# The second layer's state space preparation moves into the first layer's attention

## The reference, cut to what matters

```python
def attention(h, wq, wk, wv, wo):            # layer 0, 32 heads of 64, 8 key heads; in _L0_ffn_ref
    ...
    scores = jnp.einsum('bhqd,bhkd->bhqk', q, k) / jnp.sqrt(jnp.float32(D))
    ...
    attn = jax.nn.softmax(scores, axis=-1)
    out = jnp.einsum('bhqk,bhkd->bhqd', attn, v)
    ...
    return out @ wo

def _ssm_forward(hidden_states, z, in_proj_w, conv_w, conv_b, x_proj_w, dt_proj_w, dt_proj_b, A_log, D):
    x = jnp.einsum('ed,bld->bel', in_proj_w, hidden_states)     # layer 1; hidden_states is the context
    ...                                                          # causal convolution over 4 places
    u = jax.nn.silu(xc + conv_b[None, :, None])
    x_dbl = jnp.einsum('ke,bel->bkl', x_proj_w, u)
    dt_lo = x_dbl[:, :DR]
    Bm = x_dbl[:, DR:DR + DS]
    Cm = x_dbl[:, DR + DS:]
    delta = jax.nn.softplus(jnp.einsum('er,brl->bel', dt_proj_w, dt_lo) + dt_proj_b[None, :, None])
    A = -jnp.exp(A_log)
    ...                                                          # the scan
```

## Time and profile before

| what | us |
|---|---|
| median of three runs (lowest, highest) | 2777.11 (2775.63, 2784.5) |
| profiled execution | 2792.75 |
| its span | 2791.5 |
| TensorE busy in the span | 2100.1 (75%) |
| VectorE busy | 1581.8 (57%) |
| ScalarE busy | 1107.5 (40%) |
| GpSimd busy | 1007.5 (36%) |

### The profile page before, as it was taken

One profiled execution on the slowest core, in us unless ns is written; L12 is line 12 of the kernel. 1 busy time (PEld: TensorE's weight loads), 2 busy tenths in 40 slices (PEclk: granted clock), 3 DMA queues, 4 the chain that ended last, 5 costly groups with the idle time before them and its releaser, 6 DMA issues. The chain is left out here.

```text
span 2791.5 us, 35700 instructions
## 1 busy us (share of the span) xinstructions
PE 2100.1 (75%) x12825; PEld 1478.7 (53%) x12872; DVE 1581.8 (57%) x3073; ACT 1107.5 (40%) x2234; POOL 1007.5 (36%) x1048
## 2 busy tenths in 40 slices
PE   6676735999974888856525688878999968797755
PEld 2333313776754777743303344546888845554444
DVE  6877674444444555545687655544546555455466
ACT  3255415555432444422264144542444434312534
POOL 2766501666536656651152033321233212100012
PEclk8756767999987999988757878978999989799787
DMA  3222100000004444420100000011000000010000
GB/s 134 72 57 56 39 21 28 18 12 22 9 1 155 159 159 155 155 71 15 45 0 37 2 3 3 3 54 46 1 1 1 1 1 2 2 39 7 2 37 15
DMA packets 48431, 114.59 MB, mean 41 GB/s; under 512 B 5472, under 2 KB 18144, under 8 KB 46976
## 3 DMA queue, kind: packets, MB, share of 16 engines
q1 hardware_dynamic: 46720, 108.10, 12.0%
q0 software_dynamic: 1536, 4.20, 0.5%
HBM read 100.09 MB, written 11.14 MB: 40 GB/s over the span
## 5 line engine op out<-in xcount | busy, mean ns | idle before, releaser
L1717 POOL TENSOR_SCALAR l0f_probs<-l0f_probs,l0f_tot 128x128 f32<-128x128 f32 (+1 forms) x256 | 190.8, 766 | 134.1 <-DVE l0f_tot L1671 133.9
L1939 PE MATMUL ps<-l0f_xh,l0f_wh 128*128 128x256 f32 x480 | 147.9, 308 | 49.6 <-DVE l1x_dBu L594 28.3
L1200 DVE TENSOR_REDUCE l2a_a_max<-ps 128x6 f32<-128x768 f32 x128 | 119.4, 954 | 87.6 <-PE ps L1052 87.0
L2889 POOL TENSOR_TENSOR l2x_probs<-l2x_probs,l2x_rc 128x512 f32<-128x512 f32 x64 | 66.6, 1041 | 265.1 <-DVE l2x_rc L2804 265.1
L1256 POOL TENSOR_SCALAR_AFFINE_SELECT l2a_a_probs<-l2a_a_probs 128x256 f32<-128x256 f32 (+1 forms) x192 | 88.5, 485 | 172.8 <-ACT l2a_a_probs L1162 150.9
L2054 POOL TENSOR_TENSOR l0f_wl<-l0f_raw,l0f_wh 128x1024 fp32r<-128x1024 f32 x60 | 141.8, 2376 | 17.3 <-ACT l0f_wh L1979 17.2
L1941 PE MATMUL ps<-l0f_xh,l0f_wl 128*128 128x256 f32 x480 | 139.8, 291 | 0.0
L1601 ACT ACTIVATE l0f_probs<-ps,l0f_neg 128x128 f32<-128x128 f32 (+1 forms) x256 | 104.6, 426 | 88.3 <-DVE l0f_neg L1661 88.3
L1940 PE MATMUL ps<-l0f_xl,l0f_wh 128*128 128x256 f32 x480 | 139.5, 291 | 0.0
L619 POOL TENSOR_TENSOR l1x_y<-l1x_y,l1x_hc 128x512 f32<-128x512 f32 x64 | 80.8, 1284 | 126.4 <-DVE l1x_hc L610 126.4
L1939 PEld LDWEIGHTS ps<-l0f_xh,l0f_wh 128*128 128x128 f32 x480 | 95.4, 199 | 57.4 <-issue 31.8
(11 more groups left out here) (758 smaller groups left out, 5919.6 us busy)
## 6 DMA issues: line engine op xcount, KB each, us to landing
l0f_raw<-in_e_l0f SPq DMA_DIRECT2D x60, 512.0 KB, 3.8
l0x_bc<-scratch_bc SPq DMA_DIRECT2D x32, 512.0 KB, 4.8
l0f_raw_d<-in_e_l0f SPq DMA_DIRECT2D x60, 256.0 KB, 3.7
scratch_rows<-zero SPq DMA_DIRECT2D x1, 3840.0 KB, 19.0
l0f_xb<-scratch_rows SPq DMA_DIRECT2D x15, 256.0 KB, 4.1
scratch_results<-l0f_yb SPq DMA_DIRECT2D x15, 256.0 KB, 4.4
l0f_slab<-in_g_l0f SPq DMA_DIRECT2D x8, 448.0 KB, 3.5
l1f_raw<-in_w_l1f SPq DMA_DIRECT2D x1, 3072.0 KB, 10.2
```

What stands on the lines that cost most here:

```text
L1200: dve.tensor_reduce(M[:, 2 * half:2 * half + 2, j, :], src.rearrange("p a (c n) -> p a c n", c=NB_), AX.X, ALU.max).then_inc(*unit_max.tick())
L1717: last = pool.tensor_scalar(pr[:, u % 3, a, r], pr[:, u % 3, a, r], tot[:, u % 3, qt, a:a + 1], None, ALU.mult)
L1939: pe.matmul(out, hi, xh[:, j % 2, c, :], start=c == 0, stop=False)
```

## The change

`prepare` no longer runs as a stage. It only makes the buffers and signals, and the work is cut into pieces that the loops of `l0f_attention` call in their steps. The pieces with a matmul also take a place in the ring, as a use "P" between A and V. The pieces by step:

| steps | TensorE | ScalarE | VectorE |
|---|---|---|---|
| before -8 | | Exp of A | negate A, halve the convolution's weights |
| 0 to 3 | context projection | copy | |
| 5 to 12 | | tanh in 10 | convolution, one instruction per step |
| 13, 16 | | tanh in 14 | (tanh + 1) times x/2 |
| 18, 19 | low rank rows | copy | |
| 20 to 23 | B and C rows | | split into three parts, seven instructions |
| 25 to 28 | time steps | | bias |
| 30 to 34 | | Abs 30, 31; Exp 32, 33; both Ln 34 | |
| 36 to 39 | | | skip term and sum 36, 38; product 37, 39 |

The silu is formed as x/2 (1 + tanh(x/2)) with the halved weights instead of x / (1 + exp(-x)): Exp, add, reciprocal and product become tanh and one instruction. Abs, Exp and Ln work on halves of 1024 columns instead of quarters of 512. The buffers of the sum, u and the low rank rows now lie in buffers that the scan has anyway. The memsets and copies of GpSimd run behind its first two weight splits. One barrier goes.

```diff
+    INNER, LOW, ROWS, DT = range(4), range(18, 20), range(20, 24), range(25, 29)
+    def emptied(self, n):
+        for at, done in ((self.INNER, self.in_sb), (self.LOW, self.low_sb), (self.ROWS, self.bc_sb), (self.DT, self.dt_in)):
+            if n in at:
+                return done(n - at[0] + 1)
...
+        if n in (10, 14):
+            d = (n - 10) // 4
+            act.wait_ge(*self.conv(d + 1))
+            act.activation(self.dt[:, d], self.du[:, d], ACT.Tanh).then_inc(*self.tanh.tick())
...
+        if n == 34:
+            for d in range(2):
+                act.wait_ge(*ac(d + 4))
+                act.activation(self.dt[:, d], self.dt[:, d], ACT.Ln, bias=1.0).then_inc(*self.dt_ln.tick())
...
+        if n in (13, 16):
+            d = (n - 13) // 3
+            dve.wait_ge(*self.tanh(d + 1))
+            dve.scalar_tensor_tensor(self.du[:, d], self.dt[:, d], 1.0, self.du[:, d], ALU.add, ALU.mult).then_inc(*self.u_ok.tick())
...
+        if n in self.ROWS:
...
+            dve.wait_ge(*self.bc_ps(i + 1))
+            dve.wait_ge(*self.cleared(9))
+            dve.tensor_copy(hb, bank[0:96, :]).then_inc(*v.tick())
+            dve.wait_ge(*v.now())
+            dve.tensor_tensor(rest, bank[0:96, :], hb, ALU.subtract).then_inc(*self.bc_sb.tick())
+            dve.tensor_copy(out[0:16], hb[0:16])
+            dve.wait_ge(*self.bc_sb(i + 1))
+            dve.tensor_copy(mb, rest).then_inc(*v.tick())
...
-        scan.prepare()
-        l0f_attention(k, h, xT)
+        l0f_attention(k, h, xT, scan)
...
-        uses += [("A", g, i) for g, i in a_of(n)] + ([("V", n - 3, 0)] if 0 <= n - 3 < N else []) + [("O", g, i) for g, i in o_of(n)]
+        uses += [("A", g, i) for g, i in a_of(n)] + scan.uses(n) + ([("V", n - 3, 0)] if 0 <= n - 3 < N else []) + [("O", g, i) for g, i in o_of(n)]
...
                 for g, i in a_of(n):
                     project(g, i)
+                for u in scan.uses(n):
+                    scan.pe_step(n, ring(*u), ring_free(*u))
                 if 0 <= n - 2 < N:
                     turn(n - 2)
...
             high(0)
+            scan.act_first()
...
+                if scan.uses(n):
+                    scan.act_step(n, ring("P", n, 0))
                 if 0 <= n < N:
                     exponent(n)
+                if not scan.uses(n):
+                    scan.act_step(n, None)
                 if 0 <= n - 2 < N:
                     take_turned(n - 2)
...
                 if 0 <= n - 2 < N:
                     take_turned(n - 2)
+                scan.dve_step(n, ring("P", n, 0) if scan.uses(n) else None)
                 for g, i in o_of(n):
                     add(g, i)
```

More of the change, by code:

```diff
@@ L412, in __init__ @@
         self.bs = [sb("bst", [P, NB, S], BF16), sb("cst", [P, NB, S], BF16)]
[L414 to L443, removed]
@@ L444, in at_pe, with pe_step @@
+    def pe_step(self, n, bank, free):
+        k, pe, w = self.k, self.k.pe, self.w
+        pe.wait_ge(*free)
+        if n in self.INNER:
+            d, hf = divmod(n - self.INNER[0], 2)
+            if n == self.INNER[0]:
                 pe.wait_ge(*k.loaded(self.wname))
                 pe.wait_ge(*k.loaded("ctx"))
[L446 to L459, removed]
@@ L543, in prepare @@
-            at_pool()
[L544 to L547, removed]
+            pe.matmul(bank, w["inp"][:, d * P:(d + 1) * P], k.ctxT[:, hf * HALF:(hf + 1) * HALF], start=True, stop=True).then_inc(*self.in_ps.tick())
+        elif n in self.LOW:
+            hf = n - self.LOW[0]
+            pe.wait_ge(*self.u_ok(2))
+            for c in range(2):
+                last = pe.matmul(bank[0:8, :], w["xw"][:, c, 0:8], self.flat(self.du, c)[:, hf * HALF:(hf + 1) * HALF], start=c == 0, stop=c == 1)
+            last.then_inc(*self.low_ps.tick())
+        elif n in self.ROWS:
+            hf, z = divmod(n - self.ROWS[0], 2)
+            pe.wait_ge(*self.cleared(9))
+            for c in range(2):
+                last = pe.matmul(bank[0:96, :], self.wr[:, c, z, :], self.flat(self.du, c)[:, hf * HALF:(hf + 1) * HALF], start=c == 0, stop=c == 1)
+            last.then_inc(*self.bc_ps.tick())
+        else:
+            d, hf = divmod(n - self.DT[0], 2)
+            pe.wait_ge(*self.low_sb(hf + 1))
+            pe.matmul(bank, w["dtw"][:, d * P:(d + 1) * P], self.low[:, hf * HALF:(hf + 1) * HALF], start=True, stop=True).then_inc(*self.dt_ps.tick())
@@ new lines, in act_first, with act_step @@
+    def act_first(self):
+        self.k.act.wait_ge(*self.k.loaded(self.wname))
+        self.k.act.activation(self.An[:, :, :], self.w["alog"], ACT.Exp).then_inc(*self.chain.tick())
+    def act_step(self, n, bank):
+        act, ac = self.k.act, self.chain
+        if n in self.INNER:
+            d, hf = divmod(n - self.INNER[0], 2)
+            act.wait_ge(*self.in_ps(n - self.INNER[0] + 1))
+            act.copy(self.xp[:, d, 2 * hf:2 * hf + 2, 3:3 + S], bank.rearrange("p (b s) -> p b s", s=S)).then_inc(*self.in_sb.tick())
+        if n in (10, 14):
+            d = (n - 10) // 4
+            act.wait_ge(*self.conv(d + 1))
+            act.activation(self.dt[:, d], self.du[:, d], ACT.Tanh).then_inc(*self.tanh.tick())
+        if n in self.LOW:
+            hf = n - self.LOW[0]
+            act.wait_ge(*self.low_ps(hf + 1))
+            act.copy(self.low[:, hf * HALF:(hf + 1) * HALF], bank[0:8, :]).then_inc(*self.low_sb.tick())
+        if n in (30, 31):
+            d = n - 30
+            act.wait_ge(*self.dt_in(2 * d + 2))
+            act.activation(self.dt[:, d], self.t(d), ACT.Abs).then_inc(*ac.tick())
+        if n in (32, 33):
+            d = n - 32
+            act.wait_ge(*ac(d + 2))
+            act.activation(self.dt[:, d], self.dt[:, d], ACT.Exp, scale=-1.0).then_inc(*ac.tick())
+        if n == 34:
+            for d in range(2):
+                act.wait_ge(*ac(d + 4))
+                act.activation(self.dt[:, d], self.dt[:, d], ACT.Ln, bias=1.0).then_inc(*self.dt_ln.tick())
```

159 lines of the change are left out of this document (77 added, 82 removed).

## The result

| what | us |
|---|---|
| before, median of 4 runs (lowest, highest) | 2778.66 (2775.63, 2784.5) |
| after, median of 4 runs (lowest, highest) | 2741.39 (2737.8, 2747.87) |
| ratio, 95% interval | 0.986 (0.9844 to 0.9876) |
| profiled execution after, its span | 2741.67, 2740.4 |

The changed kernel is 37 us faster. I had forecast 2731 us with a range of 2714 to 2750; the measured median lies 1.4 us above the narrower 2722 to 2740 that I had given to my own mechanism. Steps repeat from one execution to another to 0.05 us, except where TensorE's clock falls.

A forecast was written before the change was run, and what follows sets the result against it. Preparation was taken as a chain of engines waiting for each other, attention as bound by TensorE. 70.8 us go and 25.1 come back (17.8 - 4.1 + 5.2 + 2.3 + 3.9): -45.7 from 2777.1, so 2731 us, range 2714 to 2750.

The forecast's parts named there:

- old stage gone: Preparation ahead of the attention: nothing else runs there, so all of its 70.8 us lie on the path and go.
- context projection in 0 to 3, less the waits filled: Attention steps 0 to 3: four projections of 0.89 us each, with 2.0 us taken as filling TensorE's waits; +1.5 us.
- low rank pieces in 18, 19, less the wait filled: Attention steps 18 and 19: two pieces of 1.78 us each on TensorE, filling a wait of 0.96; +2.6 us.
- time step pieces in 25 to 28, less the waits of 24 and 27: Attention steps 25 to 28: pieces of 0.89 us each on TensorE, filling waits of 0.22 and 0.96; +2.4 us.
- waits for the bank: Back projection waits for the piece's bank: 1.35 us in steps 20, 21, 22 and 0.55 in 27, 28; +5.2 us.
- Ln ahead of the copy in 34: Step 34, ScalarE: table load and two Ln delay the copy of the turned probabilities, so TensorE waits; +2.3 us.
- lock between VectorE and GpSimd: Steps 8, 11, 40 and 17: VectorE instructions with two SBUF operands block GpSimd's multiplications through a shared port pair; +3.9 us.
- TensorE pays for each record: Attention, bound by TensorE: 20 inserted matmuls are 40 records of 0.444 us at full clock, all counted; +17.8 us.
- Waits filled: Attention steps 0 to 3, 19, 25 and 27: inserted pieces partly fill waits TensorE already had; -4.1 us.
- Rival (a): GpSimd becomes the attention's bound: 18.1 us of pushes in place of 3.9, so -31.5 us, 2746 us; chance 0.15.
- Rival (b): Pieces slip wholly into the attention, ring waits and step 34 covered: 13.7 us back, -57 us, 2720 us; chance 0.17.
- Rival (c): TensorE's clock drops from step 20 to the attention's end: -46 + 235 us, kernel slower at 2966 us; chance 0.03.

The follow-up runs named there:

- the combination: Changed kernel with both Ln in step 35, bank emptied first, two-SBUF-operand pieces moved and sixteen warming matmuls at the head: 2730.94 us, ratio 0.9826 to before.

## Why the prediction was right

| step of the prediction | forecast | measured |
|---|---|---|
| old stage gone | -70.8 | -70.8 |
| context projection in 0 to 3, less the waits filled | +1.5 | +0.6 |
| low rank pieces in 18, 19, less the wait filled | +2.6 | +2.8 |
| B and C pieces in 20 to 23 | +7.1 | +7.1 |
| time step pieces in 25 to 28, less the waits of 24 and 27 | +2.4 | +3.5 |
| waits for the bank | +5.2 | +4.6 |
| Ln ahead of the copy in 34 | +2.3 | +2.3 |
| lock between VectorE and GpSimd | +3.9 | +2.2 |
| clock behind the waits of 11 and 35 | 0 | +3.3 |
| head; clock at the end | 0 | +1.1; -2.7 |
| sum | -45.7 | -46.0 |

That the sums agree to 0.3 us is partly luck. The terms that I had too low miss by 5.7 us (low rank pieces, time steps, clock, head), those that I had too high by 5.9 (context projection, bank, lock, clock at the end), and the last of these is a chance of one execution of the kernel before.

1. *The stage is on the path and goes whole*: right. In the mean of the traces the attention starts 73 us earlier, 2 more than the stage, since the work ahead ended a little earlier too.
2. *TensorE pays for each record*: right, 0.444 us per record (a matmul as the trace lists it), shown by steps 20 to 23. The time steps' matmul is the exception, mis-sized by 1.1 to 1.3 us: the price came from matmuls of 128 rows one behind the other, and standing so, the 8-row ones had cost the same. Between 128-row matmuls they cost 0.3 us more.
3. *Waits filled*: right for 19, 24 and 27. The context projections cost 0.6 instead of 1.5; more of them lay in waits than I had counted.
4. *Waits for the bank*: right in place, cause and nearly in size (1.16 for 1.35; 0.60 and 0.51 for 0.55). Emptying the bank first took all of it away.
5. *Ln in step 34*: right to 0.1 us; what I had not put into the sum is the clock behind the wait. Nor had I the head: I saw there a gain of 1.6 us at best, and it lost 1.1, since 14 projections instead of 8 ran at the low clock.
6. *The lock*: the mechanism is shown, its places were half right. Steps 11 and 40 paid 0.82 and 0.77 instead of 1.28 and 1.25, step 7 paid 0.6 and step 8 nothing: the piece of step 6 runs beside the multiplications that step 7 waits for. I had charged the piece's whole length. In steps 11 and 40 GpSimd had no slack, but lost only part of it, in one multiplication that had begun after the piece had (1.75 and 1.69 us instead of 0.92); in step 7 it lost 1.1 (2.00 us) and slack took some of that.
7. Rival (a), GpSimd as the bound at 2746 us, lies nearer to the timed medians than my 2731, but not for its reason: TensorE waits for GpSimd 12.8 us, less than the 16.1 before. Rival (b) fell with the bank waits. Rival (c) was right in kind and far off in size: the clock fell for a few microseconds at each of two waits and came back, 3.3 us and not 235.

What failed is the last line of the working, "2777.1 - 45.7": the path changed by 46 us and the timed runs by 37 (34 the second time). It stayed inside the range since that had been made wide for (a) and the runs' spread.

## What to carry to other kernels

Before work is slipped into another stage, price it where it lands: each record of the bound engine in full, and for every inserted piece ask who empties its buffer and how many instructions stand ahead of that one; putting the emptying instruction first gave 4.5 us for free. An engine with half its time free can still not take one long instruction, so cut or replace it (the two reciprocals of 6.6 us would have cost 11.2). And separate what a rewrite of the arithmetic brings from what the move brings: here the first was 20 of the path's 46 us. The timed gain can differ from the path's by several microseconds (37 or 34 against 46 here), and why it did is open.

## What the runs showed of the hardware

- A piece of two matmul records over 8 rows costs TensorE 0.3 us more than one over 128 rows of the same 512 columns, when it stands between matmuls of 128 rows. One behind the other, eight of either kind took the same (3.69 and 3.67 us).
- The granted clock fell behind single waits of 1.78 us (step 11, in four of the eight traces that have it) and 3.27 us (step 35, in six of eight), for some 1.6 us each; behind the three waits of 1.16 us it never did.
- At the head, sixteen matmuls in TensorE's idle time let the first projections run at full clock, 3.0 us less. In the combination they took 3.6 us and a wait of 2.5 us followed; in the run with them alone they took 5.4 us, part of it at the low clock, and a wait of 0.7.
- In the changed kernel a single multiplication of GpSimd took up to 2.10 us beside VectorE's pieces, 0.93 at most before. Beside a scalar-tensor-tensor of 1.22 us it lost 0.77, beside a reduction of 1.21 us nothing.
